# First attention of a four-layer kernel: small steps in other slots, projections four batches ahead, weights loaded in eight pieces

## What is computed

```python
projected = jnp.einsum('bte,fe->btf', query, in_proj_weight)      # q, k, v
q = q / jnp.sqrt(8)
attention = jnp.einsum('bhtd,bhkd->bhtk', q, k) + mask            # causal
x = jnp.einsum('bhtk,bhkd->bhtd', softmax(attention), v)
out = jnp.einsum('bte,fe->btf', x, out_proj_weight)
x = _layernorm(query + out)        # then: expert layer, windowed attention, expert layer
```

## Time and profile before

| | us |
|---|---|
| median of 3 executions | 1040.7 (1027.12 to 1043.34) |
| the profiled execution | 1030.89, of it a span of 1029.2 |
| first attention in that execution | from 0 to 347.5 |

### The profile page before, as it was taken

How to read it: one execution, slowest core, us unless ns; L and a number is a source line. 1 busy time by engine, 2 the same in 40 slices (tenths; PEclk the granted TensorE clock), 3 DMA queues, 4 the chain that set the end, 5 groups by cost and what they waited for, 6 DMA issues and landing times. The chain is left out here.

```text
span 1029.2 us, 17916 instructions
## 1 busy us (share of the span) xinstructions
PE 688.9 (67%) x5665; PEld 475.6 (46%) x5666; DVE 478.6 (47%) x1623; ACT 341.8 (33%) x715; POOL 383.3 (37%) x590
## 2 busy tenths in 40 slices
PE   1877788777786301999388898988322374898840
PEld 1344445444444201999256666665222353556520
DVE  4665455676652200333166556555355695222204
ACT  1144444555555000455155444444100000231214
POOL 2144344444434075332444333431200002577763
PEclk9888788999988555999587777778555555597875
DMA  5439433334320311122111111110100001133335
GB/s 146 81 71 293 107 59 69 86 70 90 71 43 7 92 46 48 57 66 64 50 37 40 40 34 35 42 32 21 26 0 0 0 1 52 50 77 58 70 28 163
DMA packets 80295, 62.31 MB, mean 61 GB/s; under 512 B 14905, under 2 KB 71906, under 8 KB 79970
## 3 DMA queue, kind: packets, MB, share of 16 engines
q1 hardware_dynamic: 72546, 52.89, 20.1%
q0 software_dynamic: 7680, 8.53, 4.5%
HBM read 36.88 MB, written 24.25 MB: 59 GB/s over the span
## 5 line engine op out<-in xcount | busy, mean ns | idle before, releaser
L508 DVE TENSOR_REDUCE a_mx<-a_psR 128x6 f32<-128x768 f32 x128 | 120.8, 955 | 90.8 <-PE a_psR L288 90.7
L436 ACT ACTIVATE a_pr<-a_psR 128x768 f32<-128x768 f32 x128 | 103.6, 810 | 121.6 <-PE a_psR L301 120.6
L232 POOL TENSOR_SCALAR_AFFINE_SELECT a_pr<-a_pr 128x512 f32<-128x512 f32 x128 | 81.3, 635 | 167.6 <-ACT a_pr L436 167.6
L806 DVE TENSOR_TENSOR e_hT<-e_hr 128x512 f32<-128x512 f32 x40 | 27.7, 693 | 100.1 <-ACT e_hr L775 100.1
L935 POOL TENSOR_TENSOR a_rs<-a_ve,mhalf 128x2 f32<-128x2 f32 x32 | 23.1, 721 | 132.4 <-DVE a_ve L1176 132.4
L280 PE MATMUL a_psR<-a_maskA,identb 128*128 128x256 bf16 x256 | 54.7, 299 | 19.1 <-DMA a_ks<-qkd 19.1
L1528 POOL DMA_INDIRECT acc<-e_ot,e_ixa x32 | 50.3, 1570 | 19.6 <-issue 7.3
L1598 ACT ACTIVATE e_yT<-e_psX,e_lb,e_lw 128x512 f32<-128x512 f32 x8 | 6.2, 775 | 153.8 <-PE e_psX L1619 153.8
L313 PE MATMUL a_psO<-a_pr,a_va 128*32 128x256 f32 x512 | 48.5, 457 | 3.5 <-POOL a_pr L232 3.5
L1503 POOL COPY e_ixg<-ids 128x4 int32<-128x4 int32 x8 | 3.7, 468 | 125.2 <-POOLq L1238 125.2
L298 PE MATMUL a_psR<-a_qs,a_ks 50*128 50x256 bf16 x256 | 37.1, 290 | 16.3 <-DVE a_mx L508 12.0
(11 more groups left out here) (263 smaller groups left out, 1727.1 us busy)
## 6 DMA issues: line engine op xcount, KB each, us to landing
qkd<-a_hml SPq DMA_DIRECT2D x16, 384.0 KB, 2.8
e_w<-in_fc SPq DMA_DIRECT2D x16, 256.0 KB
a_qs<-qkd SPq DMA_DIRECT2D x32, 96.0 KB
a_ks<-qkd SPq DMA_DIRECT2D x32, 96.0 KB
xs<-zero SPq DMA_DIRECT2D x1, 2560.0 KB, 12.3
e_xt<-xs SPq DMA_DIRECT2D x40, 64.0 KB, 1.8
ys<-e_yt SPq DMA_DIRECT2D x40, 64.0 KB, 1.5
a_qs<-qkd SPq DMA_DIRECT2D x32, 64.0 KB
```

The source lines that it names most:

```text
L232: g.affine_select(out=diagonal, in_=diagonal, pattern=[[0, 4], [1, 128]], compare_op=ALU.is_ge, fill=0.0, base=0, channel_multiplier=-1).t ...
L436: a.activation(pr[s][:, :, 0:3, :].rearrange("p x k q -> p x (k q)"), psR[:, r:r + 2, 0:384], ACT.Exp).then_inc(probs, 1)
L508: v.tensor_reduce(mx[b % 2][:, :, u, :], psR[:, r:r + 2, 0:384].rearrange("p x (k c) -> p x k c", c=128), AX.X, ALU.max).then_inc(a_max, 1)
```

## The change

Names of the stages of a step are now P = i + 4, V = i + 1, B = i, F = i - 1 and G = i - 2: the projection of q and k runs one batch further ahead, with a fifth stack, and the residual, the statistics and the normalisation of a batch come one step later than its output projection. In detail:

- The small steps have other slots. PE: q and k of P in slot 0, the halves x = 0 and x = 1 of the second weighing in slots 1 and 2, values of V in slot 3, transposed maxima in slot 4, the first weighing in slots 5 and 6, output projection by halves in slots 6 and 7.
- The residual is no longer a product with an identity. The 136 columns of that product become 8 (router columns only), and DVE adds the rows `xall`, loaded by two DMAs of 1 MB, while it moves `psM` to a tile `y`. Statistics and `x1` read `y`.
- The maxima are joined by one `tensor_reduce`, transposed in float32 (two products), and split into halves by ACT (`mhi`) and DVE (`mlo`) after the transposition. Four DMAs of 4 KB put the rows into the stack instead of two of 8 KB.
- On each engine other than PE a slot's small steps stand ahead of its exponential or maximum, except ACT's `x1`, which stands behind it in slot 3.
- SP's order is: parts of P out, `x1` of G out, rows of V, stacks of P in; the two large pieces of `xT` are issued after the stacks in steps -3 and -2; `preload` goes out in eight pieces in steps 2 to 9.
- At the start, the large memsets move from DVE to POOL, and the first product waits for `xT` and `wq` alone. There are 22 steps (-4 to 17) instead of 20 (-3 to 16).

```diff
-        NQ = 4
+        NQ = 5
...
+        def stages(i):
+            return [batch(i + ahead) for ahead in (4, 1, 0, -1, -2)]
+
         def max_unit(i, s):
-            b = batch(i + 1 if s < 4 else i + 2)
-            return None if b is None else (b, s + 4 if s < 4 else s - 4)
-
-        STEPS = range(-3, NB + 1)
+            b = batch(i + 1 if s < 3 else i + 2)
+            return None if b is None else (b, s + 5 if s < 3 else s - 3)
+
+        STEPS = range(-4, NB + 2)
...
-                P, F = batch(i + 3), batch(i - 1)
-                R = batch(i + 1)
-                if R is not None:
-                    sp.wait_ge(mT_sb, R + 1)
-                    for x in range(2):
-                        r = 64 * x + 48
-                        sp.dma_start(qs[R % NQ][r:r + 2, :, :], mrow[R % 2][32 * x:32 * x + 32, :]
-                                     ).then_inc(rows_in[R % NQ], 16)
+                P, V, B, F, G = stages(i)
                 if P is not None:
+                    if P >= 2:
+                        sp.wait_ge(stack_in[(P - 2) % NQ], 16 * 12 * ((P - 2) // NQ + 1))
                     sp.wait_ge(qk_high, P + 1)
                     sp.wait_ge(qk_low, P + 1)
-                    if P >= 2:
-                        sp.wait_ge(stack_in[(P - 2) % NQ], 16 * 12 * ((P - 2) // NQ + 1))
                     sp.dma_start(qkd[P % 2].rearrange("c r f t -> f (c r) t"), hml[P % 2][:]).then_inc(hml_out[P % 2], 16)
+                if G is not None:
+                    sp.wait_ge(x1_sb, G + 1)
+                    sp.dma_start(x1v[G], x1[G % 2][:]).then_inc(x1_out[G % 2], 16)
+                if V is not None:
+                    for parts, ready, a in ((mhi, mhi_sb, 0), (mlo, mlo_sb, 1)):
+                        sp.wait_ge(ready, V + 1)
+                        for h in range(2):
+                            r = 64 * h + 48 + a
+                            sp.dma_start(qs[V % NQ][r:r + 1], parts[V % 2][:, h, :]
+                                         ).then_inc(rows_in[V % NQ], 16)
+                if P is not None:
                     sp.wait_ge(hml_out[P % 2], 16 * (P // 2 + 1))
                     if P >= NQ:
                         sp.wait_ge(s_ps, HP * (P - NQ + 1))
                     else:
                         sp.wait_ge(ks_set, 1)
                     load_stacks(P)
-                if F is not None:
-                    sp.wait_ge(x1_sb, F + 1)
-                    sp.dma_start(x1v[F], x1[F % 2][:]).then_inc(x1_out[F % 2], 16)
-                if i == 1:
-                    preload(sp)
+                if i in (-3, -2):
+                    lo, hi = CHUNKS[i + 5]
+                    sp.dma_start(xT[:, T * lo:T * hi], xT_in[:, T * lo:T * hi]).then_inc(xT_in_sem[i + 5], 16)
+                if i in (-1, 2):
+                    c = 0 if i < 0 else 1
+                    rows = slice(NT // 2 * c, NT // 2 * c + NT // 2)
+                    sp.dma_start(xall[:, rows, :], x.rearrange("(n p) d -> p n d", p=128)[:, rows, :]).then_inc(x_in[c], 16)
+                if 2 <= i < 2 + E8:
+                    preload(sp, i - 2)
...
-                B, F, P = batch(i), batch(i - 1), batch(i + 3)
+                P, V, B, F, G = stages(i)
                 for s in range(HP):
-                    if B is not None:
-                        causal(B, s)
-                    if s == 3 and P is not None:
+                    if s == 2 and P is not None:
                         pool.wait_ge(qk_rest, P + 1)
                         g.tensor_copy(hml[P % 2][:, 1:5:3, :], rest[:]).then_inc(qk_mid, 1)
                         pool.wait_ge(qk_mid, P + 1)
                         g.tensor_tensor(hml[P % 2][:, 2, :], rest[:, 0, :], hml[P % 2][:, 1, :], ALU.subtract)
                         g.tensor_tensor(hml[P % 2][:, 3, :], rest[:, 1, :], hml[P % 2][:, 4, :], ALU.subtract
                                         ).then_inc(qk_low, 1)
-                    if s == 6 and F is not None:
-                        pool.wait_ge(ve_sb, F + 1)
-                        if F >= 1:
-                            pool.wait_ge(x1_sb, F)
+                    if B is not None:
+                        causal(B, s)
+                    if s == 2 and G is not None:
+                        pool.wait_ge(ve_sb, G + 1)
+                        if G >= 1:
...
             def max_mask(b, u):
                 if u == 0:
+                    pe.wait_ge(consts, 1)
                     pe.wait_ge(stack_in[b % NQ], 16 * 12 * (b // NQ + 1))
                 wait_banks_free(pe, a_max, (b, u))
                 r = banks(a_max, (b, u))
                 for x in range(2):
-                    o = psR[:, r + x, 0:384].rearrange("p (k c) -> p k c", c=128)
-                    mm(o[:, 0:3:2, :], identb[:], maskA[:], start=True, stop=True)
+                    mm(psR[:, r + x, 128:384], identb[:], maskA[:], start=True, stop=True)
...
+            def out_project(b, t):
+                tokens = slice(128 * t, 128 * t + 128)
+                o = psM[:, 256 * t:256 * t + D + 8]
+                mm(o[:, D:D + 8], xT[:, T * b + 128 * t:T * b + 128 * t + 128], wrc[:], start=True, stop=True)
+                return mm(o, onT[:, tokens], won[:], start=False, stop=True, skip_group_check=True)
...
+                    if s == 0 and P is not None:
+                        pe.wait_ge(xT_in_sem[chunk_of[P]], 16)
+                        if G is not None:
+                            pe.wait_ge(y_sb, G + 1)
+                            pe.wait_ge(lg_sb, G + 1)
+                        elif B is not None:
+                            pe.wait_ge(mlo_sb, B + 1)
+                        elif P >= 1:
+                            pe.wait_ge(qk_rest, P)
+                        for c in range(2):
+                            last = mm(psM[:, T * c:T * c + T], wq[:, D * c:D * c + D], xT[:, T * P:T * P + T], start=True,
+                                      stop=True)
+                        last.then_inc(qk_ps, 1)
...
+                    if s in (1, 2) and F is not None:
+                        if s == 1:
+                            pe.wait_ge(on_sb, 2 * F + 1)
+                            pe.wait_ge(masked, HP * F + HP)
+                        weigh_values(F, 1, s - 1)
+                    if s == 3 and F is not None:
+                        o_transpose(F, 1)
+                    if s == 3 and V is not None:
+                        if P is not None:
+                            pe.wait_ge(qk_rest, P + 1)
                         else:
-                            pe.wait_ge(qk_high, 2)
-                            pe.wait_ge(qk_rest, 2)
+                            pe.wait_ge(y_sb, G + 1)
+                            pe.wait_ge(lg_sb, G + 1)
...
+                        pe.wait_ge(m_sb, V + 1)
+                        pe.wait_ge(v_sb, V + 1)
+                        for h in range(2):
+                            last = tr(psM[0:2 * HP, 128 * h:128 * h + 128], mx[V % 2][:, h, 34:50])
+                        last.then_inc(mT_ps, 1)
...
+                    if s in (6, 7) and F is not None:
+                        if s == 6:
+                            pe.wait_ge(onT_sb, F + 1)
+                            if V is not None:
+                                pe.wait_ge(mlo_sb, V + 1)
+                            elif G is not None:
+                                pe.wait_ge(y_sb, G + 1)
+                                pe.wait_ge(lg_sb, G + 1)
+                        last = out_project(F, s - 6)
+                        if s == 7:
+                            last.then_inc(y_ps, 1)
...
+                    if s == 4 and V is not None:
+                        act.wait_ge(v_ps, V + 1)
+                        if V >= 3:
+                            act.wait_ge(pv_done, 2 * (V - 3) + 2)
+                        else:
+                            act.wait_ge(va_set, 2)
+                        a.copy(va[V % 3][:].rearrange("p n (x r) -> p n x r", x=2)[:, :, :, 0:DH0].rearrange("p n x r -> p x n r"),
+                               psM[:, 0:T].rearrange("p (x n d) -> p x n d", x=2, d=DH0)).then_inc(v_sb, 1)
...
+                    if s == 3 and G is not None:
+                        act.wait_ge(nr_sb, G + 1)
+                        if G >= 2:
+                            act.wait_ge(x1_out[G % 2], 16 * (G // 2))
                         for t in range(2):
-                            ins = a.activation(x1[F % 2][:, t, :], psM[:, 256 * t:256 * t + D], ACT.Identity,
-                                               bias=nr[:, t, :], scale=rs[:, t, :])
+                            ins = a.activation(x1[G % 2][:, t, :], y[:, t, :], ACT.Identity, bias=nr[:, t, :],
+                                               scale=rs[:, t, :])
                         ins.then_inc(x1_sb, 1)
...
+            def residual(b):
+                dve.wait_ge(y_ps, b + 1)
+                dve.wait_ge(x_in[2 * b // NB], 16)
+                if b >= 1:
+                    dve.wait_ge(x1_sb, b)
```

(71 more changed lines are left out.)

267 lines of the change are left out of this document (97 added, 170 removed).

## The result

| | before | after |
|---|---|---|
| median, us | 1042.0 of 4 executions | 990.5 of 4 (984.95 to 994.1) |
| the profiled execution | 1030.89, span 1029.2 | 987.88, span 986.2 |
| end of the first attention in it | 347.5 | 305.6 |
| what follows | 681.7 | 680.6 |

The ratio is 0.9575, 95% interval 0.944 to 0.971: faster; it compares the executions in the faster of two clock states alone, and so lies nearer to 1 than 990.5 / 1042.0. The program behind the stage end is the same in all kernels, but took 672 to 689 us in the profiled executions of this document, so stage ends tell more of the change than totals do.

What follows compares the result with a forecast made beforehand. No engine was full; PE, nearest to full, lost 4.4 us a step to waits, plus 1.3 to clock and DMAs. Forecast: 48 + 14 x 16.4 + 42 = 320 us against 347.5, hence 1003, median 1004, range 970 to 1032.

Steps and rivals of the forecast that it cites:

- the central case: The forecast's own case for the whole kernel: 990 to 1020 us, median 1004, chance 0.5.
- PE's work, 12.7 us: PE's work in a new step without waits, summed from old starts: 12.7 us, the same as before.
- Waits that go: PE's waits for x1 before the values (1.46 us) and for the split of the maxima (1.05 us) disappear.
- the bounds: DVE's joining tensor_reduce, whose price was not in the trace: between nothing and 0.5 us.
- The wait that comes: PE stands 2.4 us in slot 4 for POOL's parts, scale, x1, value copy: chain 5.8 us, cover 3.4.
- DVE, 0.4: PE's wait in slot 2 for DVE's maximum of slot 1: 0.4 us a step, between none and 0.75.
- DMAs and clock, 0.9 a step: Average loss per step beyond 15.5 us: 0.9 us left for the clock; the 4.33 us rows wait should not return.
- Start, 48 us: Start of the stage at 48 us instead of 45, as xT and batch 3's parts precede batch 0's rows on SP.
- 14 x 16.4: The stage's middle: 14 steps at a mean of 16.4 us, between the 48 us start and 42 us end.
- No stall: Rival: the 2.4 us stall in slot 4 does not form; step 13.4 us, 958 in all, chance 0.15.
- A clock that falls in every step: Rival: half clock behind the slot 4 stall costs 2.7 us; 18.2 us a step, 1028 in all, chance 0.2.
- Late rows: Rival: maxima rows reach PE late in every step; 19.4 us a step if landing takes 5 us, 1045, chance 0.05.

Runs made afterwards that it cites:

- the POOL move: The changed kernel with POOL's scale and shift of batch G put ahead of the three parts of batch P in slot 2; 953.8 us, ratio 0.922.

## Why the prediction was right

**The end result.** 990.5 lies within 970 to 1032, 1.3% under 1004, and just at the lower edge of the 990 to 1020 of the central case. Against the profiled execution the sum said 28 us less, and 43 came, so the gain was put at two thirds of what it was.

**PE's work, 12.7 us.** It holds: in the step with a 0.55 us wait the distance is 13.33, 12.8 without it, and the identity product makes no difference.

**Waits that go.** They went; the join takes 0.20 us, within the bounds.

**The wait that comes.** 2.4 us forecast, 2.44 measured, with the releasers named; removing and lengthening the chain moved it as the sum would have it. This is the best step of the forecast: all its terms were rows of a trace in which the chain did not exist.

**DVE, 0.4.** A full-clock step is 15.2, so 0.1 is left for it. PE waits for DVE's maxima 2.4 us in all.

**DMAs and clock, 0.9 a step.** No step waits 4.33 us for rows after the preload. The mean over the ten steps from 82.24 to 244.88 is 16.3, as forecast (16.4), which owes something to luck: the clock's share was scaled, not derived. Eight fallen steps at 1.5 us are 12 us, 0.9 a step over 14: the clock fell in more steps than the one in three that 0.9 at the rival's price of 2.7 us means, and each fall cost little more than half of that price.

**Start, 48 us.** 47.3. PE waits 8.6 us for the rows of batch 0, which stand behind parts, stacks and `xT`.

**The term that was mis-sized** is "14 x 16.4". Steps 0 and 1 have no batch G, so no `x1`: 12.9 us from the copy of step 0 to that of step 1. From step 12 on there is no batch P, so no parts stand before the scale on POOL, the wait before the transposed maxima is 1.1 us in place of 2.4 in steps 12 and 13, and the last three distances are 15.4, 13.9 and 13.9 us. The mean of the 14 is 15.6, and 14 x 0.8 = 11 of the 14 us that the stage ended earlier than forecast (305.6 against 320) lie there, 9.5 of them in these four distances. The start gave 1 of the rest and the end 2: from the start of step 14 at 265.69 us it took 39.9, not 42.

**Rivals.** No stall: did not come by itself, but is what the POOL move makes, at 954. A clock that falls in every step: eight of ten, and all ten with 0.7 us more of stall, so this rival came nearer than its chance of 0.2 says; it was its price that was too high. Late rows: issue of the four DMAs ends at 199.85, 4.3 us before PE's scores at 204.11, where the forecast had about 2; no wait in most steps. The start of the next step is covered by the stall itself, so a kernel without the stall comes nearer to that wait: the POOL move shows 4.5 us of it in all steps together.

## What to carry to other kernels

When small steps move to other slots, follow each bank and tile through all engines: a wait removed on one engine comes back where two independent pieces of work meet on another in the wrong order, here parts ahead of scale on POOL. Its length can be computed from old rows, chain less cover. Check at both ends of the pipeline which steps hold the whole chain, and put large transfers into pieces when small urgent ones share their queue.

## What the runs showed of the hardware

- Behind the preload in one piece, 6.6 MB in three DMAs, issuing a pair of DMAs of 4 KB held SP for 8.0 us, where some 1.2 us is usual. That a full queue is the reason is my reading; no row shows it.
- With nearly the same work in a step, a gap of 2.4 us went with a fallen clock in eight of ten steps, one of 3.1 us in ten, one of 1.4 or 0.55 us in none. The kernel before, with gaps of at most 1.5 us, has steps at 1.00 and steps at 0.81 to 0.83.
- A reduction of 32 to 16 elements took DVE 0.20 us, where the comparison of two strided tiles of 16 that it replaced took 0.51.
